# Head means and head denominators of the q, k, v stage on ScalarE, and VectorE's sums of squares at the head of its turn

## The reference, cut to what matters

```python
h = _layernorm(x) * (1 + ca) + sa                 # per row, 512 columns
q = _layernorm(h, qn_g, qn_b) @ Wq + bq           # k, v likewise from kvn and Wkv
q = _rotary(q * hd ** (-0.25), h)                 # turns pairs of columns, times |h| of the row
mu = mean(q over a head); var = mean((q - mu) ** 2)
qn = (q - mu) * rsqrt(var + 1e-5) * ln_g + ln_b   # per head of 32 columns
```

## Time and profile before

| | us |
|---|---|
| median of 3 runs (2519.64 to 2523.82) | 2522.72 |
| the profiled execution: time | 2521.72 |
| its span | 2519.8 |
| the q, k, v stage in it: last step of `factor` ends | 390 |

### The profile page before, as it was taken

How to read it: one execution, slowest core, us unless ns; L and a number is a source line. 1 busy time by engine, 2 the same in 40 slices (tenths; PEclk the granted TensorE clock), 3 DMA queues, 4 the chain that set the end, 5 groups by cost and what they waited for, 6 DMA issues and landing times. The chain is left out here.

```text
span 2519.8 us, 33443 instructions
## 1 busy us (share of the span) xinstructions
PE 2316.9 (92%) x12520; PEld 1706.0 (68%) x12520; DVE 1170.1 (46%) x1799; ACT 792.5 (31%) x1671; POOL 743.2 (29%) x823
## 2 busy tenths in 40 slices
PE   6999992899999999999858799999999999999998
PEld 4777771656655665665446587887878787878787
DVE  5999984655555555555269612212121213121212
ACT  3333331244454554454435411111111111111111
POOL 2667773011111111111167222222222222222221
PEclk8999995699999999999989899999999999999999
DMA  6122224643554365443179521212121211212111
GB/s 218 68 100 100 100 92 122 140 101 99 129 135 111 96 144 127 103 99 81 36 248 299 196 68 34 84 34 83 33 80 36 65 51 46 71 46 71 44 56 33
DMA packets 162369, 244.24 MB, mean 97 GB/s; under 512 B 17188, under 2 KB 84356, under 8 KB 161760
## 3 DMA queue, kind: packets, MB, share of 16 engines
q1 hardware_dynamic: 153760, 221.71, 30.2%
q0 software_dynamic: 7456, 18.07, 2.6%
q10 hardware_dynamic: 1056, 3.15, 0.3%
HBM read 132.74 MB, written 59.26 MB: 76 GB/s over the span
## 5 line engine op out<-in xcount | busy, mean ns | idle before, releaser
L882 DVE TENSOR_REDUCE b_top<-b_psA 128x2 f32<-128x1024 f32 (+3 forms) x384 | 363.3, 957 | 288.8 <-PE b_psA L801 165.1
L949 ACT ACTIVATE b_probT<-b_psB 128x512 f32<-128x512 f32 (+3 forms) x768 | 339.7, 491 | 348.5 <-PE b_psB L825 233.0
L1298 DVE TENSOR_TENSOR f_gu<-f_psU,f_silu 128x512 f32<-128x512 f32 x128 | 88.5, 691 | 749.3 <-PE f_psU L1359 749.3
L822 PE MATMUL b_psB<-b_stack 98*128 98x512 f32 (+3 forms) x768 | 287.5, 413 | 7.1 <-ACT b_probT L949 5.8
L801 PE MATMUL b_psA<-b_stack 96*128 96x512 f32 (+3 forms) x768 | 256.5, 392 | 27.9 <-DMA b_stack<-b_halves 20.2
L822 PEld LDWEIGHTS b_psB<-b_stack 98*128 98x128 f32 x768 | 139.8, 188 | 190.8 <-issue 118.5
L57 POOL TENSOR_TENSOR f_spots<-f_still 1x1 f32<-1x1 f32 x128 | 25.9, 202 | 794.8 <-PE f_psD L1347 788.7
L1288 ACT ACTIVATE f_silu<-f_psG 128x512 f32<-128x512 f32 x128 | 76.6, 598 | 523.5 <-PE f_psG L1359 523.5
L1345 PE MATMUL f_psD<-f_wd_hi,f_gu_hi 128*128 128x512 f32 x512 | 201.1, 393 | 22.8 <-DVE f_gu_lo L1302 12.3
L1357 PE MATMUL f_psG<-f_hT_hi,w_hi 128*128 128x512 f32 x512 | 200.6, 392 | 10.9 <-DVE f_hT_lo L1309 10.9
L1358 PE MATMUL f_psG<-f_hT_hi,w_lo 128*128 128x512 f32 x512 | 199.9, 390 | 0.0
(11 more groups left out here) (179 smaller groups left out, 4210.2 us busy)
## 6 DMA issues: line engine op xcount, KB each, us to landing
b_stack<-b_halves SPq DMA_DIRECT2D x192, 256.0 KB, 5.0
f_wd<-in_wd_t SPq DMA_DIRECT2D x128, 256.0 KB, 2.6
qkv_d<-a_t SPq DMA_DIRECT2D x32, 512.0 KB, 2.7
b_land<-qkv_d SPq DMA_DIRECT2D x32, 512.0 KB, 4.6
a_x<-in_x SPq DMA_DIRECT2D x32, 256.0 KB, 3.3
qkv_d<-a_v SPq DMA_DIRECT2D x32, 256.0 KB, 3.0
b_v<-qkv_d SPq DMA_DIRECT2D x16, 512.0 KB, 5.9
att_d<-b_att SPq DMA_DIRECT2D x16, 512.0 KB, 3.2
```

Of the source, the lines that this page charges most:

```text
L822: mm = pe.matmul(psB[:, i % 2, cols], stack[0:NR, n % BUFS, 0, j, kb * P:(kb + 1) * P], stack[0:NR, n % BUFS, 1, j, first * P:(half + 1) * ...
L882: dve.tensor_reduce(out, slot("score", NI * n + i)[:, :, 0:width], AX.X, ALU.max, negate=True).then_inc(s["maxed"], 1)
L949: act.activation(probT[:, (NW * n + w) % 3, j, 0:width], psB[:, i % 2, 0:width], ACT.Exp).then_inc(s["expd"], 1)
```

## The change

VectorE's `means` keeps only the sum over the heads; the multiplication by -1/32 becomes `mean_heads` on ScalarE, ahead of `square_heads`. VectorE's `spread` keeps only the sum of squares over the heads and becomes the first step of VectorE's turn instead of the last. The denominator becomes `denominator` on ScalarE, its first step; the reciprocal stays on VectorE as `invert`, its last step. ScalarE squares with a scale of 32 to the power -1/2, so the sums of squares are already divided by 32, and `ms2h` goes. The lags are those of before. Two new semaphores (`vsums`, `dens`) carry the new hand-overs; `rec_ready` now counts once a tile instead of three times, and two pairs of SyncE's semaphores are merged into `rows_out`.

```diff
@@ semaphores @@
-        rows1_out, mod_in = sem("rows1_out"), sem("mod_in")
-        late_copied, late_step, late_out = sem("late_copied"), sem("late_step"), sem("late_out")
+        rows_out, mod_in = sem("rows_out"), sem("mod_in")
+        late_copied, late_step = sem("late_copied"), sem("late_step")
@@ SyncE, at the end @@
-            sp.wait_ge(late_out, 16 * 4)
+            sp.wait_ge(rows_out, 16 * 6)
@@ VectorE @@
                 dve.tensor_reduce(hsum[:, t % 4], r, AX.X, ALU.add).then_inc(s["sums"], 1)
-                dve.wait_ge(s["sums"], done(b, t))
-                dve.tensor_scalar(hmean[:, t % 4], hsum[:, t % 4], -1.0 / HD, None, ALU.mult).then_inc(s["means"], 1)
 
             def spread(b, t):
 
                 dve.wait_ge(s["squared"], done(b, t))
-                dve.tensor_reduce(vsum[:, t % 4], t1[:, t % 4].rearrange("p (h d) -> p h d", d=HD), AX.X, ALU.add)
-                dve.tensor_scalar(ms2h[:, t:t + 1], ms2[:, t:t + 1], 1.0 / HD, None, ALU.mult).then_inc(s["rec_ready"], 1)
-                dve.wait_ge(s["rec_ready"], thrice(b, t, 1))
-                dve.tensor_scalar(den[:, t % 4], vsum[:, t % 4], ms2h[:, t:t + 1], EPS, ALU.mult, ALU.add).then_inc(s["rec_ready"], 1)
-                dve.wait_ge(s["rec_ready"], thrice(b, t, 2))
+                dve.tensor_reduce(vsum[:, t % 4], t1[:, t % 4].rearrange("p (h d) -> p h d", d=HD), AX.X, ALU.add).then_inc(s["vsums"], 1)
+
+            def invert(b, t):
+                dve.wait_ge(s["dens"], done(b, t))
                 dve.reciprocal(rec[:, t % 4], den[:, t % 4]).then_inc(s["rec_ready"], 1)
 
-            stagger(dve, B, TB, [(norm_h, 3), (norm_x, 1), (stat_h, 2), (stat_x, 0), (turn, 5), (low, 3), (means, 6), (spread, 7)])
+            stagger(dve, B, TB, [(spread, 7), (norm_h, 3), (norm_x, 1), (stat_h, 2), (stat_x, 0), (turn, 5), (low, 3), (means, 6), (invert, 7)])
@@ ScalarE @@
-                act.activation(t1[:, t % 4], t2[:, t % 4], ACT.Square).then_inc(s["squared"], 1)
+                act.activation(t1[:, t % 4], t2[:, t % 4], ACT.Square, scale=float(HD) ** -0.5).then_inc(s["squared"], 1)
+
+            def mean_heads(b, t):
+                act.wait_ge(s["sums"], done(b, t))
+                act.activation(hmean[:, t % 4], hsum[:, t % 4], ACT.Copy, scale=-1.0 / HD).then_inc(s["means"], 1)
+
+            def denominator(b, t):
+                act.wait_ge(s["vsums"], done(b, t))
+                act.activation(den[:, t % 4], vsum[:, t % 4], ACT.Identity, scale=ms2[:, t:t + 1], bias=eps[:, 0:1]).then_inc(s["dens"], 1)
 
             def factor(b, t):
-                act.wait_ge(s["rec_ready"], thrice(b, t, 3))
+                act.wait_ge(s["rec_ready"], done(b, t))
                 act.activation(fac[:, t % 4], rec[:, t % 4], ACT.Sqrt, scale=ms2[:, t:t + 1]).then_inc(s["fac_ready"], 1)
 
-            stagger(act, B, TB, [(scale_x, 1), (high, 3), (root_h, 2), (root_x, 0), (take_v, 5), (square_h, 2), (square_heads, 6), (factor, 7)])
+            stagger(act, B, TB, [(denominator, 7), (scale_x, 1), (high, 3), (root_h, 2), (root_x, 0), (take_v, 5), (square_h, 2), (mean_heads, 6), (square_heads, 6), (factor, 7)])
```

More of the change, by code:

```diff
@@ L149, in qkv_stage @@
         ms2 = sb("a_ms2", [P, 8])
-        ms2h = sb("a_ms2h", [P, 8])
         hT_hi = sb("hT_hi", [P, 2, DM], F32R)
@@ L174, in qkv_stage @@
                  "turned hi_ready lo_ready qkv_mm v_ready turns_ready rotated sums means centred squared "
-                 "rec_ready fac_ready qk_ready").split()
+                 "vsums dens rec_ready fac_ready qk_ready").split()
         s = {n: sem("a_" + n) for n in names}
@@ L194, in done @@
             return b * TBn + (t + 1)
-        def thrice(b, t, n):
-            return b * (3 * TBn) + (3 * t + n)
         def first(b, t, at):
@@ L231, in load @@
                     sp.wait_ge(small_act, ACT_ROW)
-                    sp.dma_start(scratch["mod"][:, 0, :], rows1[0:B]).then_inc(rows1_out, 16)
+                    sp.dma_start(scratch["mod"][:, 0, :], rows1[0:B]).then_inc(rows_out, 16)
                     sp.wait_ge(small_dve, DVE_ROW)
-                    sp.dma_start(scratch["mod"][:, 1, :], rows1[HD:HD + B]).then_inc(rows1_out, 16)
+                    sp.dma_start(scratch["mod"][:, 1, :], rows1[HD:HD + B]).then_inc(rows_out, 16)
                 if first(b, t, 5):
-                    sp.wait_ge(rows1_out, 32)
+                    sp.wait_ge(rows_out, 32)
                     for later in range(1, B):
@@ L253, in _ @@
                 sp.wait_ge(late_copied, m - 1)
-                sp.dma_start(scratch["mod"][:, m, :], late[at, n]).then_inc(late_out, 16)
+                sp.dma_start(scratch["mod"][:, m, :], late[at, n]).then_inc(rows_out, 16)
             for j in range(4):
                 sp.wait_ge(stored[j], 32 * NT // 4)
-            sp.wait_ge(late_out, 16 * 4)
+            sp.wait_ge(rows_out, 16 * 6)
         @block.gpsimd
```

## The result

The changed kernel takes 2569.36 us, the median of 4 runs (2568.6 to 2570.83), the kernel before 2522.09: ratio 1.0189, 95% interval 1.0171 to 1.0207. It is 47 us slower. The forecast was 2570.

A forecast was written before the change was run, and what follows sets the result against it. It took VectorE's own list, 10.64 us a turn, as the bound. A new loop of 12.35 us over 26 turns plus the drain made the stage 47.7 us longer: 2521.72 + 47.7 = 2569.4, stated as 2570, range 2556 to 2588.

The forecast's parts named there:

- The bound of the kernel before: In the q, k, v stage, VectorE's own list was said to set the turn of 10.64 us.
- ScalarE's rows beside GpSimd's show none: Reading of the earlier trace: ScalarE's operations do not wait for GpSimd's, unlike VectorE's L399 and L407.
- Off VectorE: Small operations leaving VectorE's turn: 0.77 plus 1.02 us, 1.8 us saved, its list falling from 10.64 to 8.8 us.
- Rival 1: Wait ahead of L404 is short and VectorE's saving comes through: 26 us gained, 2496 us; chance 4%.
- On to ScalarE: Two 32-column operations added to ScalarE, mean 0.25 us and denominator 0.30 us, neither on the path setting the turn.
- The loop from L404 to L404: Sums of squares at VectorE's head wait on norm_x, GpSimd's four operations and ScalarE's square: 12.35 us a turn.
- The ends: Stage's start and finish: turn 7 at 68.7, turn 33 at 389.8, last L497 ending at 437.8 us.
- the drain: Last turns of the stage, from turn 33 to turn 38, together 45.7 us.
- Port rival: VectorE's 32-column reciprocal waits for GpSimd amid L277 and holds up L281: 9 us more, 2579 us; chance 12%.
- Clock rival: TensorE's clock falls in longer rests: 2570 to 2575 us if it recovers, 2746 if it stays down (3%).
- The prediction's own sign of error: A TensorE clock under 1.00 between 80 and 370 us was listed as showing the forecast wrong.

The follow-up runs named there:

- e8: Kernel before with the head mean alone moved to ScalarE, the denominator and the place of the sums of squares as before; 2515.48 us.
- e1_end: Changed kernel with sums of squares back behind the means and the denominator between ScalarE's mean and square, arithmetic still on ScalarE; 2492.62 us.
- e4: Changed kernel with GpSimd's last two steps exchanged, centre ahead of rotate; 2561.75 us.
- e3: Kernel before with its whole spread step moved to the head of VectorE's turn, all arithmetic staying on VectorE; 2599.79 us.
- e6: Changed kernel with eight more matmuls, later overwritten, ahead of each product on TensorE; 2576.41 us.
- e7: Changed kernel with sums of squares in the middle of VectorE's turn and norm_x moved behind the two statistics; 2528.62 us.

## Why the prediction was right, point by point

- **The bound of the kernel before**, put as "the stage goes at the pace of VectorE's own list", and "nothing in that turn waits for another engine's work of the same turn": this step failed. The prediction saw that L399 and L407 stand still for GpSimd and did not draw the conclusion. e8 shows that the turn was a loop through GpSimd's row and L407's wait; taking 0.77 us off VectorE gave 5 us in all, not 20. The forecast did not suffer, because the new turn was added up from starts along the loop and not from this bound.
- **"ScalarE's rows beside GpSimd's show none"** (no wait): the rows given do not show that, as all of the earlier trace rows lie where GpSimd rests (205.70 to 208.59). That it holds is shown by the changed kernel's L489, 0.23 us beside L272, and by e1_end's L493, 0.41 us beside L276 and as long where GpSimd rests (206.52 in the changed kernel).
- **Off VectorE, 1.8 us a turn; own list 8.8.** Measured 216.5 us of busy time in 317, 8.5 us in a turn of 12.40: 0.3 us less than put. Rival 1 was priced by TensorE's 9.6, as either list is shorter. e1_end showed that case: 9.61 us and 2493, for 2496 in the rival.
- **On to ScalarE.** The mean was put at 0.25 and took 0.23; the denominator at 0.30 and took 0.41. Neither was on the path, as said: e4 found the mean 0.45 us behind the path, for 0.5. The Trainium skill, "ScalarE: Activation LUTs", section "What ACT_TABLE_LOAD costs", gives 186 ns plus 0.833 a column, and some 93 for each per-partition operand. The estimates by it are 0.21 and 0.40 us; the trace agrees (0.23 and 0.41), and for the denominator it is closer than the 0.30 put from L497's row.
- **The loop from L404 to L404.** 12.35 put, 12.40 measured. The steps in order: 1.14 for 1.13, 1.01 for 0.97, 1.59, 3.26, 2.37 for 2.36, 1.93 for 1.95, 1.10 for 1.09. Over 26 turns (68.43 to 391.48) the mean is 12.43, 2 us in all. e1 and e3 show that the place makes the loop, whichever engine does the arithmetic, and e4 that it ran through GpSimd.
- **The ends.** Turn 7 at 68.43 for 68.7, turn 33 at 391.48 for 389.8, the drain 46.04 for 45.7, the end 439.93 for 437.8. The stage became 49.9 us longer for 47.7; that the whole came to 47 is owed to 3 us gained behind the stage, in the projection above all, which no step had and whose cause stays open. The agreement of 2569.4 with 2570 to within 1 us is in that part luck.
- **Port rival.** Refuted: L401 takes 0.34 us beside L272.
- **Clock rival.** "In the rows the clock was full until TensorE had rested 4.8 us" was too thin a ground: in the changed kernel it fell after as little as 2.0 us of rest. That a burst which begins at half clock would stay within the turn of the loop was right, and e6 shows it. The prediction's own sign of error, a clock under 1.00, did appear, and was no error in the time.

## What to carry to other kernels

In a stage of staggered lists, a step that is moved ahead across the turn's boundary keeps its lag but loses a turn of slack (here 77 to 80 us): add up the chain from the step's place back to itself through every engine, in-order neighbours included, before looking at busy shares. Operations of VectorE that share ports with GpSimd hide their waits in their own length (0.82 us for 0.24 in the kernel before); compare each with the same form where GpSimd rests, or the "busy" engine will be taken for the bound. An independent reduction was worth most here where it covered GpSimd's operation: the same two reductions exchanged cost 18 us.

## What the hardware showed beyond what was expected

- VectorE's two-input L341 takes 0.75 us alone and 2.12 beside L276; L362 takes 0.55 alone and up to 3.07; the denominator's tensor_scalar of 32 columns 0.24 alone and 1.52. The reciprocal of 32 columns (0.34) and the reductions (1.2) did not wait beside GpSimd in any run (0.33 to 0.35 and 1.16 to 1.22).
- A waiting L362 got in between two GpSimd operations that follow each other in seven turns of e7 and waited through both in 17 (206.47 to 209.54, for one), from about the same point of the first.
- TensorE's granted clock fell to half in or just behind rests of 2.6 to 2.8 us in eight turns (after as little as 2.0 us) and stayed full through such rests in six.
